# Second attention of a four-layer kernel: rotary halves exchanged on ScalarE, matmuls in quarter tiles of the array, softmax division one chunk later

## The reference

```
q_c    = LN(x) @ W_dq                       # (2, 512, 96)
kv_c   = ctx @ W_kvc                        # (2, 128, 64)
q_rope = rope((q_c @ W_qr) as 16 heads x 64)   # [x1 cos - x2 sin, x1 sin + x2 cos], halves of 32
k_rope = rope(kv_c @ W_kr)
scores = (q_nope . k_nope + q_rope . k_rope) / sqrt(192)   # 16 heads
scores = where(seg - 8 <= k <= seg, scores, -1e30)
out    = (softmax(scores) @ v) @ W_o        # q_nope = q_c @ W_uq, k_nope = kv_c @ W_uk, v = kv_c @ W_uv
x      = x + out
gate, up = silu(q(x, wq_gate)), q(x, wq_up) # 704 hidden units, weights (w - 128) * scale
x      = x + q(gate * up, wq_down)
```

## Time and profile before

| what | before |
|---|---|
| median of 3 runs | 863.61 us (861.7 to 863.77) |
| the profiled execution | 862.67 us |
| its span | 860.9 us |
| PE busy in the span | 810.3 us (94%) |
| DVE, ACT, POOL busy | 661.2, 521.0, 457.1 us |
| chain that ended last | PE 66%, DVE 21%, ACT 9%, issue 3% |

### The profile page before, as it was taken

How to read it: one execution, slowest core, us unless ns; L and a number is a source line. 1 busy time by engine, 2 the same in 40 slices (tenths; PEclk the granted TensorE clock), 3 DMA queues, 4 the chain that set the end, 5 groups by cost and what they waited for, 6 DMA issues and landing times.

```text
span 860.9 us, 14397 instructions
## 1 busy us (share of the span) xinstructions
PE 810.3 (94%) x4888; PEld 692.9 (80%) x4888; DVE 661.2 (77%) x1584; ACT 521.0 (61%) x1202; POOL 457.1 (53%) x776
## 2 busy tenths in 40 slices
PE   3777999999999999999899999999999999999998
PEld 2566888888888888888788788988888878777887
DVE  7988888899888998879988894955544758876534
ACT  6888877788678886788764645433322334646332
POOL 2485869779685996858953864252010028760000
PEclk9779999999999999999999999999999999999999
DMA  7000120012101030000100416947310000100001
GB/s 236 14 1 1 38 74 1 2 38 61 51 1 32 7 111 1 2 1 22 47 25 14 148 38 181 232 138 270 105 52 23 11 34 25 50 1 1 0 2 49
DMA packets 28376, 45.99 MB, mean 53 GB/s; under 512 B 3952, under 2 KB 18096, under 8 KB 28176
## 3 DMA queue, kind: packets, MB, share of 16 engines
q1 hardware_dynamic: 26800, 41.31, 16.4%
q10 hardware_dynamic: 1504, 3.77, 1.2%
HBM read 43.89 MB, written 1.18 MB: 52 GB/s over the span
## 4 chain that ended last, share of the span: by engine, by line
PE 66%; DVE 21%; ACT 9%; issue 3%; DMA 1%; SPq 0%; ACTq 0%; DVEq 0%
PE PS L760 18%; PE PS L829 8%; PE PS L716 5%; PE PS L621 5%; PE PS L652 4%; PE PS L690 4%; PE PS L930 3%; DVE cat L1498 3%; PE PS L885 2%; PE PS L662 2%; PE PS L643 2%; DVE yb L1494 2%; PE PS L673 2%; PE PS L920 2%; PE PS L700 2%
## 5 line engine op out<-in xcount | busy, mean ns | idle before, releaser
L2166 POOL TENSOR_SCALAR raw<-raw,mvq,rsq 128x128 f32<-128x128 f32 x312 | 187.6, 615 | 7.2 <-DVE mvq L1639 5.7
L760 PE MATMUL PS<-xq,WH 128*128 128x512 f32 x480 | 151.0, 396 | 0.0
L760 PEld LDWEIGHTS PS<-xq,WH 128*128 128x128 f32 x480 | 87.8, 190 | 17.0 <-issue 0.8
L760 PE MATMUL PS<-xq,WL 128*128 128x512 f32 x240 | 94.1, 392 | 0.0
L621 PE MATMUL PS<-WH,xq 128*128 128x256 f32 (+1 forms) x256 | 89.6, 367 | 3.6 <-issue 1.5
L621 PE MATMUL PS<-WL,xq 128*128 128x256 f32 (+1 forms) x256 | 84.9, 349 | 0.0
L1086 ACT ACTIVATE P<-PS,sm 128x256 f32<-128x256 f32 x128 | 60.7, 492 | 31.1 <-DVE sm L1667 30.9
L1592 DVE BATCH_NORM_STATS2 st<-raw 128x6 f32<-128x128 f32 x320 | 71.9, 276 | 0.9 <-ACT raw L1058 0.9
L829 PE MATMUL PS<-xq,m_hh 128*128 128x256 f32 x384 | 69.3, 281 | 1.4 <-DVE m_hl L1956 0.6
L716 PE MATMUL PS<-PH,cat 128*128 128x256 f32 x256 | 64.7, 292 | 6.2 <-DVE cat L1498 5.9
L690 PE MATMUL PS<-PT,vr 128*128 128x256 f32 x256 | 66.2, 381 | 1.0 <-ACT PT L972 1.0
(11 more groups left out here) (299 smaller groups left out, 2208.7 us busy)
## 6 DMA issues: line engine op xcount, KB each, us to landing
wst<-in_wgu SPq DMA_DIRECT2D x24, 256.0 KB, 3.7
l_KM<-share SPq DMA_DIRECT2D x16, 384.0 KB, 4.0
wst<-in_wall SPq DMA_DIRECT2D x18, 256.0 KB, 3.1
l_KM<-share SPq DMA_DIRECT2D x16, 256.0 KB, 4.8
dst<-in_wdn SPq DMA_DIRECT2D x24, 128.0 KB, 3.6
wst<-in_wkvx SPq DMA_DIRECT2D x8, 256.0 KB, 3.4
l_KM<-share SPq DMA_DIRECT2D x16, 128.0 KB, 4.1
m_pre<-in_wo ACTq DMA_DIRECT2D x1, 2048.0 KB, 10.1
```

Of the source, the lines that this page charges most:

```text
L760: t = e.matmul(PS[:, b, :], W[wi][:, gu, k, :], a[:, k, cols], start=(n == 0), stop=(n == 5))
L2166: t = e.tensor_scalar(v, v, mvq[:, par, n, 0:1], rsq[:, par, n:n + 1], ALU.add, ALU.mult)
```

## The change

1. Queries: `wqr` holds the columns of a pair of heads as first halves of both, then second halves of both, and `wrt` is gone. A bank `("qr", bb, u)` now holds the plain queries of two pairs. ACT copies the two partition halves crosswise into `tqs`, with a minus sign (`swap_q`), then DVE multiplies the bank with the cosines into `tqc`, which empties it, and `tqs` with the sines in place; POOL adds 512 columns at a time. Two buffers of each kind. The qr banks are 6, 7, 2, 3 for block 0 and 6, 7 by turns for the others.
2. Tiles: `keymix` works in pairs of 64-row tiles into two banks; `absorb` alternates between output partitions 0 to 63 and 64 to 127; `values2` uses four 64x64 tiles of `BDK`, which now holds the keys in all four quarters, for two banks at a time; the keys `kc` are made on both halves of the partitions.
3. Order: TensorE does the queries of a step ahead of its scores, and one part more ahead of the loop; values, turn_p and project come a step later; DVE divides chunk n-1 in step n, after soft(n) and before turn_q; three buffers `S` and `s16`; the loop has 12 steps.
4. FFN: the 64 gate rows and 64 up rows of piece 5 share one bank of six matmuls, and its down matmuls contract 64 rows.

```diff
-QUERIES = {0: (2, 3), 1: (4,), 2: (5,), 3: (6,), 4: (7,)}
+QUERIES = {0: (3,), 1: (4,), 2: (5,), 3: (6,), 4: (7,)}
...
-            for part in range(2):
-                do("queries", 0, part)
-    for n in range(11):
+        for part in ((0, 0), (0, 1)) if a == 0 else ((1, 0),):
+            do("queries", *part)
+    for n in range(12):
+        for m in QUERIES.get(n, ()):
+            do("queries", m // 2, m % 2)
         if n < 8:
             do("scores", n)
-        if n % 2 and n > 2:
-            do("values", (n - 3) // 2)
-        for m in QUERIES.get(n, ()):
-            do("queries", m // 2, m % 2)
         if n % 2 == 0 and n > 3:
-            do("project", (n - 4) // 2)
-        if 0 < n < 9:
-            do("turn_p", n - 1)
-        if n % 2 == 0 and n > 5:
-            do("f_turn", (n - 6) // 2)
-        if n > 8:
-            do("f_front", *FFN[n - 9])
+            do("values", (n - 4) // 2)
+        if 1 < n < 10:
+            do("turn_p", n - 2)
+        if n % 2 and n > 4:
+            do("project", (n - 5) // 2)
+        if n % 2 and n > 6:
+            do("f_turn", (n - 7) // 2)
+        if n > 9:
+            do("f_front", *FFN[n - 10])
...
+            elif key[0] == "qr":
+                B.fill(key, (6, 7, 2, 3)[key[2]] if key[1] == 0 else 6 + key[2] % 2)
...
 # keymix
+                for y in range(4):
+                    banks = [fill(("km", 2 * y + o)) for o in range(2)]
+                    emptied(("aw", y))
+                    for i in range(2):
+                        for o, b in enumerate(banks):
+                            rows = slice(64 * o, 64 * o + 64)
+                            t = e.matmul(PS[0:96, b, i * 256:(i + 1) * 256], AT[rows, 2 * y + i, :], KA[rows, :],
...
 # values2
-                for z in range(4):
-                    b = fill(("lv", bb, z))
-                    e.matmul(PS[:, b, :], BDK[:, bb, :], PT1[:, 2 * z:2 * z + 2, :].rearrange("p a b -> p (a b)"),
-                             start=True, stop=True).then_inc(full[b], 1)
+                for z in (0, 2):
+                    banks = [fill(("lv", bb, z + i)) for i in range(2)]
+                    for r, c, i in ((0, 0, 0), (64, 64, 0), (0, 64, 1), (64, 0, 1)):
+                        t = e.matmul(PS[c:c + 64, banks[i], :], BDK[r:r + 64, bb, c:c + 64],
+                                     PT1[r:r + 64, 2 * (z + i):2 * (z + i) + 2, :].rearrange("p a b -> p (a b)"),
+                                     start=True, stop=True)
+                        if r:
+                            t.then_inc(full[banks[i]], 1)
...
 # f_front
-                for gu in range(2):
+                for gu in range(2 if j < 5 else 1):
...
 # ScalarE
+            def swap_q(bb, part):
+                for u in range(2 * part, 2 * part + 2):
+                    n = 4 * bb + u
+                    b = w.filled(("qr", bb, u))
+                    if n > 1:
+                        w.wait_ge(added.sem, added.at[(n - 2) // 4, (n - 2) % 4])
+                    e.activation(tqs[u % 2][0:64, :], PS[64:128, b, :], ACT.Copy, scale=-1.0)
+                    copy(tqs[u % 2][64:128, :], PS[0:64, b, :]).then_inc(swapped.sem, 1)
...
+            for n in range(12):
+                for m in QUERIES.get(n, ()):
+                    swap_q(m // 2, m % 2)
+                if n % 2 == 0 and n > 3:
+                    take_lv((n - 4) // 2)
+                if 1 < n < 10:
+                    take_lp(n - 2)
                 if n < 8:
                     exps2(n)
...
 # VectorE, turn_q
+                    w.wait_ge(swapped.sem, swapped.at[bb, u])
+                    e.tensor_tensor(two[0], q, cos, ALU.mult).then_inc(free[b], 1)
+                    e.tensor_tensor(two[1], two[1], sin, ALU.mult).then_inc(turned_q.sem, 1)
...
+            for n in range(12):
                 if n < 8:
                     soft(n)
+                if 0 < n < 9:
+                    scale(n - 1)
                 for m in QUERIES.get(n, ()):
                     turn_q(m // 2, m % 2)
-                if n in (5, 7):
-                    add_l((n - 5) // 2)
-                if n < 8:
-                    scale(n)
-                if n == 9:
-                    add_l(2)
+                if n in (6, 8, 10):
+                    add_l((n - 6) // 2)
...
 # GpSimd, add_q
+                    w.wait_ge(turned_q.sem, turned_q.at[bb, u])
+                    e.tensor_tensor(QR[bb % 2][:, 2 * u:2 * u + 2, :].rearrange("p a b -> p (a b)"), tqc[n % 2], tqs[n % 2],
                                     ALU.add).then_inc(added.sem, 1)
```

More of the change, by code:

```diff
@@ L724, in keys @@
                 for k in range(2):
-                    t = e.matmul(PS[0:64, b, 0:256], wkvc[:, k, :], ctxT[:, k, :], start=(k == 0), stop=(k == 1))
+                    for o in (0, 64):
+                        t = e.matmul(PS[o:o + 64, b, 0:256], wkvc[:, k, :], ctxT[:, k, :], start=(k == 0), stop=(k == 1))
                 t.then_inc(full[b], 1)
@@ L1152, in take_keys @@
                 b = w.filled("kc")
-                copy(KA[0:64, :], PS[0:64, b, 0:256]).then_inc(free[b], 1)
+                copy(KA[:, :], PS[:, b, 0:256]).then_inc(free[b], 1)
                 b = w.filled("bk")
@@ L1166, in place_keys @@
                 k23 = K2[:].rearrange("p (a t) -> p a t", a=4)
-                for o in (0, 64):
-                    copy(KZ[o:o + 64, :, o // 64, :], k23[o:o + 64]).then_inc(keys_in, 1)
+                for o in range(0, 128, 32):
+                    copy(KZ[o:o + 32, :, o // 32 % 2, :], k23[o:o + 32]).then_inc(keys_in, 1)
             def early(j, h):
@@ L1398, in scalar @@
                 take_qc(a + 1)
+                for part in ((0, 0), (0, 1)) if a == 0 else ((1, 0),):
+                    swap_q(*part)
             def gate_f(n):
@@ L1405, in gate_f @@
                     w.wait_ge(downed_f.sem, downed_f.at[FFN[n - 3]])
+                if j == 5:
+                    e.activation(fsg[n % 3][0:64, :], PS[0:64, b, :], ACT.Silu, scale=fsc[0:64, 5:6]).then_inc(gated_5.sem, 1)
+                    return
                 e.activation(fsg[n % 3][:], PS[:, b, :], ACT.Silu, scale=fsc[:, j:j + 1]).then_inc(free[b], 1)
@@ L2034, in scale @@
             def scale(c):
-                i = c % 2
+                i = c % 3
                 s3 = S[i][:].rearrange("p (h t) -> p h t", h=16)
@@ L2058, in split_f @@
                                 xq[0][:, :, cols].bitcast(F32), ALU.subtract).then_inc(free[b], 1)
-            for part in range(2):
-                turn_q(0, part)
+            for part in range(3):
+                turn_q(part // 2, part % 2)
             def gate_f(n):
                 j, h = FFN[n]
+                if j == 5:
+                    w.wait_ge(gated_5.sem, gated_5.at[h])
+                    b = w.filled(("fg", j, h))
+                    e.scalar_tensor_tensor(fsg[n % 3][0:64, :], PS[64:128, b, :], fsc[0:64, 11:12], fsg[n % 3][0:64, :],
+                                           ALU.mult, ALU.mult).then_inc(free[b], 1)
+                    return
                 w.emptied(("fg", j, h))
@@ L2301, in gpsimd @@
             w.filled(("bp", 3))
-            for part in range(2):
-                add_q(0, part)
+            for part in range(3):
+                add_q(part // 2, part % 2)
             for n in range(5):
```

157 lines of the change are left out of this document (78 added, 79 removed).

## The result

The changed kernel took 882.42 us (median of 5 runs, 875.43 to 884.69) against 863.77 us before (5 runs): a ratio of 1.0209, 95% interval 1.0172 to 1.0245. That is 18.7 us or 2% slower, 14 us above the forecast of 868.0 and outside its range of 852 to 874.

A forecast was written before the change was run, and what follows sets the result against it. VectorE was taken to set chunks 1 to 4, TensorE's own work the pace from chunk 5 on. Terms 1.1 - 2.2 - 1.2 = -2.3 us, plus 7.2 for the clock, gave +4.9 and 868.0 us, range 852 to 874.

The forecast's parts named there:

- the clock's term: Late stage: six idle stretches of TensorE each lower its clock, at 1.2 us apiece: +7.2 us.
- the start: Keymix to scores(0): scores(0) start at 706.9 instead of 705.2 us, +1.7 us, though 7 us of TensorE work is gone.
- Coupled steps: Chunks 0 to 4: TensorE and VectorE wait for each other, 11.0 us a step; scores(4) end 3.8 us later.
- Absorb: Absorb's two bursts of 1.53 us could be halved: -1.2 us, bounds 0 and -1.5.
- Values: Attention values in four tiles: 2.0 us a block instead of 3.67, 1.7 us less a block.
- rival 3: Values tiles don't run four abreast: 873 us if two at once, up to 880 in turns at a bank; chance 0.13.
- Drain: First attention's row tiles: changing tiling mode drains TensorE, seen in the 0.2 to 0.3 us beyond half of 1.77.
- FFN: FFN fronts: each half front saves 1.37 us, the first in full, of the last 0.8 is left: -2.2 us.
- Exponentials: Chunk steps on VectorE: the 1.60 us idle wait for ScalarE's exponentials goes, replaced by a longer round trip with TensorE.
- Wait of turn_p(7): After scores(4): TensorE's turn_p(7) waits from 786.8 to 789.8 us, 2.9 us, for chunk 7's softmax.
- Rival 1: Late stage: steps are coupled but TensorE's clock stays up, about 861 us; chance 0.20.
- Rival 2: Chunk steps: the round trip is covered, a step is VectorE's busy 7.7 us, total 851 us; chance 0.22.

The follow-up runs named there:

- run 1: Changed kernel plus matmuls that nobody reads at the six places where TensorE waits: 868.5 us, ratio 1.0057.
- second profile: Profile from running the changed kernel once more without an edit: 883.03 us, ratio 1.0212; profiled span 882.1 us.
- Run 2: Changed kernel plus matmuls that nobody reads in steps 1 to 4 only: 872.41 us, ratio 1.0103.
- run 4: Changed kernel with the queries put back behind scores(n) on TensorE: 858.28 us, ratio 0.9941.
- run 6: Changed kernel, order kept, queries in four banks (6, 7, 4, 5), the rest up to scores(4) in banks 0 to 3: 862.1 us, ratio 0.9983.
- run 5: Changed kernel, order kept, queries of blocks 1 to 3 in the round of banks 0 to 5: 880.7 us, ratio 1.0198.
- run 11: Changed kernel with queries behind scores, plus unread matmuls before the compression of block 2 and before turn_p(7): 858.2 us, ratio 0.9929.
- run 12: Changed kernel with four query banks and earlier x copies: queries behind scores 861.27 us, ahead of scores 857.14, the latter with four filler matmuls 856.98.
- run 8: Changed kernel with the whole order of before and two score buffers; exchange, tiles and shorter FFN piece stay: 871.38 us, ratio 1.0093.

## Why the prediction went wrong, step by step

Direction and mechanism held; the sum was too small, in the clock's term most of all. The late stage in pieces, from the first keymix matmul, in us. The first column is the prediction's sum without its clock term; the clock's 7.2 stood beside it.

| from, to | predicted, clock up | filled (run 1) | first profile | second profile |
|---|---|---|---|---|
| keymix, second mask of chunk 0 | 25.7 | 29.4 | 29.8 | 30.0 |
| to that of chunk 1 | 8.2 | 8.5 | 8.5 | 11.2 |
| to that of chunk 4, three steps | 33.0 | 33.7 | 40.2 | 41.1 |
| to the end of FFN's second front | 61.2 | 62.8 | 64.4 | 64.4 |
| to the end of the span | 47.0 | 47.4 | 47.4 | 47.3 |
| sum | 175.1 | 181.8 | 190.3 | 194.0 |

(In the kernel before the same stretch is 860.9 - 684.68 = 176.2; the -1.2 for absorb lies ahead of it. The ends are read from lines as shown above; for the first profile they are 683.32, 713.14, 721.68, 761.90, 826.26 and 873.6.)

**The step that failed is the clock's +7.2.** The same six stretches cost 194.0 - 181.8 = 12.2 us in a usual execution by the traces, and 882.4 - 868.5 = 13.9 by the medians, and the 1.8 us of clock that run 1 still has come on top. The price per stretch was too low: the earlier trace rows gave 3.5 us at a mean of 0.57, a loss of 1.5, of which I took 1.2. In the steps the lower level held for 6.8 us (0.50 from 738.7 to 745.5, for instance), from within the idle time to the first scores, and all of PE's work in it is on the path: queries 3.78 us instead of 1.89, and scores slower behind them. Run 2 prices it at 10.0 us by the medians; in the traces the three long steps took 41.1 against 33.7 and the one before them 11.2 against 8.5. I had written that "a part hides where bank 7 is waited for anyway"; in the steps, a round trip in which each engine waits for the other, nothing did: in the first profile the slowed queries and scores add up to 6.7 us, and the three steps are 6.5 us longer than in run 1.

Two readings behind that term were off as well. The idle stretch at 411 us lasted 1.84 us, not 1.5 (the matmul behind it starts at 412.74). And the clock of the kernel before fell a fourth time after 20 us, with PE busy:

```profile
476.00:480.00 4.00, 3.78 (x31) 3.48 (x29) 1.49 (x3) 2.65 (x4) 3.64 (x5) 1.00 0.97 385
480.00:484.00 4.00, 4.00 (x15) 3.20 (x15) 3.44 (x5) 2.51 (x4) 3.92 (x5) 0.65 0.36 132
```

PE has no idle stretch of 0.3 us or more in the 20 us before it. Filling the six idle stretches took the falls behind them away and left one other (run 1). So such stretches do bring falls, but a fall doesn't need one of 2 us.

**The second miss is the start, 3.7 us.** I let ScalarE take x of block 2 some 14.9 us after keymix began; it did at 16.2, and in run 1 compression ended 1.4 us later than in my sum (18.7 against 17.3). The copy stood behind swaps that waited 1.70 and 0.70 us for POOL, whose second sum waited for a sine product slowed to 1.45 us. Another 1.8 us are the lower clock that run 1 has in this piece, and 0.5 were not taken apart. Smaller misses: 1.6 us up to FFN's second front, 1.0 of them a wait of front(0) for banks that ScalarE still copies from (idle 0.95 us), which I hadn't seen; 0.3 and 0.7 us in the steps.

The sum again with what was measured: -2.3, misses at an unchanged clock 181.8 - 175.1 = 6.7, clock 12.2 to 13.9: 16.6 to 18.3 above 863.6, thus 880.2 to 881.9. Measured 882.4. With the 1.8 us put where they belong, the clock is 14.0 to 15.7 us against my 7.2, and the other terms together were short by 4.9.

What held:

- *Coupled steps.* 11.0 us predicted, 11.2 with the clock up. Right in mechanism (runs 4 and 6 remove the bank's wait from either side, and both bring the step to 8.5) and in size.
- *Absorb.* Predicted -1.2. A burst is shorter by half (0.88 us against 1.53), but the start of keymix varies by 4.8 us between executions, so that its share of the time can't be shown.
- *Values.* 2.0 us a block predicted, 1.88 measured, with 3.67 before:

```profile
761.87 1.88 PE PS L933 x16
```

  Four tiles do run abreast, and rival 3 is refuted. The Trainium skill (TensorEngine Tiling (Array Packing), Gotcha 1: PSUM Pressure) says that different row tiles cannot access the same bank at the same time; here two row tiles write one bank, on partitions 0 to 63 and 64 to 127, at 0.12 us a record against 0.46 before, which leaves no room for turns. The measurement decides for this case, in which the column tiles differ as well.
- *Drain.* The 0.2 to 0.3 us that I read as a drain are 0.1 at most: a timeline counts the end of the last matmul, which the chain leaves out (the eight matmuls of L901 are 1.05 us at 705.90 in the timeline and 0.89 in the earlier trace rows).
- *FFN.* -2.2 predicted; from the second front on 47.4 us against 49.2 before, -1.8.
- *Exponentials.* The wait of 1.60 us is gone, as predicted.
- *Wait of turn_p(7).* 2.9 us predicted, 3.27 measured.

Rival 1 (clock stays up) named the alternative rightly, and run 1 shows how it would have looked: even then 868.5, not 861. Rival 2 asked for a step of 7.7 us with the round trip covered; run 4 has it, at 8.5 and 858.3 us, by two lines of order.

## What to carry to other kernels

When a step moves ahead of another, look up which bank, buffer or semaphore it takes and how far back on the other engine that is released. A step that takes what its predecessor of one round ago still holds turns two pipelined engines into a ping-pong; count the fills of a round before choosing banks, since a round as long as a step changes nothing (run 5).

Price an idle stretch of PE inside such a coupled loop at its length plus the slowed work behind it, here 2.2 to 2.7 us a stretch; where VectorE set the pace, taking falls away brought no gain that the medians show (runs 11 and 12), and 0.8 and 1.5 us from keymix on in single profiles. Matmuls that nobody reads are a cheap test of it: they leave the waits alone and take the clock's part away.

Relieving the busiest engine (PE, 13.8 us less) was worth 1.5 us by the medians. In run 4 the steps are set by VectorE, which the relief doesn't touch, and the work went to ScalarE, on whose queue the softmax's exponentials stand: in the old order they wait for it (run 8).

## What the hardware showed beyond expectation

- The same idle time doesn't always have the same effect. After 2.80 us the clock stood at 1.00 in one profile and at 0.50 in the other. The Trainium skill (TensorE: Matmul & The Clock Gate, What's actually happening) says that the monitor behind the gate runs free of the kernel, so that the same kernel can show it differently from run to run; these two profiles agree. The stretches of 4.45 to 5.4 us were followed by 0.50 in both. An idle stretch of 1.84 us far ahead of the change, which ends at 410.77 and 412.38 us, was followed by 1.00 at 412 to 418 us in the first profile and by 0.64 at 412 to 414.5 in the second.
- Falls differ in length: the clock was at 0.50 for 6.8 us in the steps, but for 3.4 us at turn_p(7) (800.1 to 803.5 us, first profile), so that one price for all stretches doesn't fit.
- ScalarE's copy of 64 partitions by 512 took 0.59 us, about the same as a 128 x 512 one (0.60 for a single one in run 1, 1.09 for two): half the partitions save nothing. The exchange in halves costs two full copies, 1.2 us a bank.
- VectorE's product with all operands in SBUF took 0.68 us alone and up to 1.45 beside POOL, where I had allowed 0.6 to 0.9. In the steps this falls on the second sine product almost every time, as POOL adds right after the first one.
- Stages ahead of the change, equal in all these kernels, ended 4.8 us apart in two executions of the same kernel. The clock has a part in it: between 70 and 680 us the later one had it below 1.00 at 76 to 84, 412 to 418 and 496 to 500 us, the other at 478 to 484 us alone. A difference of 5 us between two single profiles says little; from one fixed instruction to the end it can be read.
